# Attribute gathers that add onto cleared places, 52 of them ahead of the first network's gathers

## The reference, cut to what matters

```
x = _layernorm(x + _L0_gnn_ref(x, ...))   # graph transformer, two layers, per-edge attention
x = _layernorm(x + _L1_gnn_ref(x, ...))   # attention by leaky_relu, summed by source node
x = _layernorm(x + _L2_gnn_ref(x, ...))   # two hypergraph convolutions (four hops)
x = _layernorm(x + _L3_gnn_ref(x, edge_attr_4, edge_attr_10, ...))
```

```
out0 = alpha * (einsum(s0 * a0, w_00_0) + inv_sqrt3 * einsum(s1, a1, w_11_0))
out1 = alpha * (einsum(s0, w_01_1, a1) + einsum(s1 * a0, w_10_1))
messages = concat([out0, out1]) * msg_rad
agg = segment_sum(messages, edge_dst)
```

## Time and profile before

| | before |
|---|---|
| median of three runs | 5668.25 us |
| the profiled execution, its own time | 5646.56 us |
| its span | 5645.4 us |
| busy PE, DVE, ACT, POOL | 3618.7, 2869.4, 1858.3, 3438.4 us |
| mean granted TensorE clock | 0.81 |

### The profile page before, as it was taken

One profiled execution on the slowest core, in us unless ns is written; L12 is line 12 of the kernel. 1 busy time (PEld: TensorE's weight loads), 2 busy tenths in 40 slices (PEclk: granted clock), 3 DMA queues, 4 the chain that ended last, 5 costly groups with the idle time before them and its releaser, 6 DMA issues.

```text
span 5645.4 us, 59886 instructions
## 1 busy us (share of the span) xinstructions
PE 3618.7 (64%) x15291; PEld 2680.2 (47%) x15291; DVE 2869.4 (51%) x6725; ACT 1858.3 (33%) x5462; POOL 3438.4 (61%) x3085
## 2 busy tenths in 40 slices
PE   4554443667964444599794666621116999968887
PEld 3433232445653232366563444411005888767776
DVE  6465567886434454788532667622002322434445
ACT  1243344663333343577231111100001010146655
POOL 4466667888886666788887666677771000046664
PEclk8876677998986666799896888865558999979988
DMA  7688885663258888576424666621004878846665
GB/s 259 198 288 279 281 289 152 161 161 50 22 119 276 287 278 288 134 169 141 71 20 76 174 168 179 173 31 20 11 11 142 262 228 276 251 142 178 178 175 141
DMA packets 688351, 951.03 MB, mean 168 GB/s; under 512 B 230789, under 2 KB 479668, under 8 KB 687880
## 3 DMA queue, kind: packets, MB, share of 16 engines
q1 hardware_dynamic: 419634, 538.30, 31.0%
q0 software_dynamic: 251600, 385.84, 28.1%
q10 hardware_dynamic: 16774, 23.00, 1.2%
HBM read 727.03 MB, written 219.80 MB: 168 GB/s over the span
## 4 chain that ended last, share of the span: by engine, by line
issue 26%; PE 23%; POOL 19%; DVE 11%; another core or an unknown queue 10%; DMA 6%; SPq 3%; ACT 1%; DVEq 1%; ACTq 0%; POOLq 0%
PE bank L2650 10%; POOL arena L927 6%; POOL sc L950 6%; POOL ATT L964 6%; PE bank L2775 6%; PE bank L2772 4%; DMA ATT<-arena 3%; DMA sc<-arena 2%; SPq L620 2%; DVE arena L1376 2%; DVE arena L1746 2%; DVE arena L1466 2%; DVE arena L1352 1%; PE bank L2490 1%
## 5 line engine op out<-in xcount | busy, mean ns | idle before, releaser
L927 POOL DMA_INDIRECT arena<-KVT,arena x832 | 801.4, 963 | 480.5 <-issue 280.3
L2490 PE MATMUL bank<-arena 128*128 128x264 f32 x1664 | 598.5, 512 | 659.8 <-issue 366.1
L927 POOL DMA_INDIRECT arena<-YT,arena x416 | 405.7, 975 | 932.6 <-DMA YT<-arena 721.6
L2490 PEld LDWEIGHTS bank<-arena 128*128 128x128 f32 x1664 | 384.9, 248 | 872.8 <-issue 663.6
L964 POOL DMA_INDIRECT ATT<-arena x391 | 644.1, 1647 | 125.1 <-issue 110.0
L950 POOL DMA_INDIRECT sc<-arena x391 | 641.6, 1641 | 125.1 <-issue 111.5
L1466 DVE TENSOR_TENSOR arena<-arena,bank 128x256 f32<-128x256 f32 x832 | 297.5, 413 | 564.5 <-remote 360.9
L927 POOL DMA_INDIRECT arena<-X1T,arena x416 | 412.0, 990 | 243.5 <-issue 126.1
L2447 PE MATMUL bank<-arena 128*128 128x273 f32 x1664 | 455.1, 412 | 141.5 <-DVE arena L1525 94.5
L2631 PE MATMUL bank<-arena 128*128 128x261 f32 x832 | 315.8, 530 | 293.9 <-DVE arena L1376 158.2
L980 POOL DMA_INDIRECT arena<-ATTR,arena x416 | 416.4, 1001 | 139.7 <-issue 139.7
(11 more groups left out here) (333 smaller groups left out, 6661.0 us busy)
## 6 DMA issues: line engine op xcount, KB each, us to landing
VE<-arena SPq DMA_DIRECT2D x208, 512.0 KB
arena<-VE SPq DMA_DIRECT2D x208, 512.0 KB
left<-ATT SPq DMA_DIRECT2D x250, 320.0 KB
left<-AM SPq DMA_DIRECT2D x250, 320.0 KB
ATT<-arena POOLq DMA_DIRECT2D x25, 1600.0 KB, 6.6
arena<-LOCT SPq DMA_DIRECT2D x312, 128.0 KB
arena<-ATT SPq DMA_DIRECT2D x75, 384.0 KB
AM<-arena SPq DMA_DIRECT2D x100, 256.0 KB
```

The lines of the kernel that those rows point to most:

```text
L927: GP.indirect_dma_start(out=ring[:, i % n, k, :], out_offset=None, in_=table, in_offset=bass.IndirectOffsetOnAxis(ap=idx[:, 4 * i + k:4 * ...
L2490: mm = P.matmul(b_[:, 0:264], OHQ[:, i % 3, k * 128:(k + 1) * 128], QS[:, i % 4, k, :], start=True, stop=True)
```

## The change

Every attribute gather becomes an adding one (`compute_op=ALU.add`) with a bounds check. For this DVE clears columns 2 to 5 of `PA` once, right after the edge number has been copied out of column 2. The gathers are cut in two: the first 52 columns are issued before POOL's waits for l1, behind the 391 counting DMAs; the other 364 stay where all 416 were.

```diff
+EARLY = 52
@@ pool_engine
+        def add_attributes(cols):
+            for c in cols:
+                GP.indirect_dma_start(
+                    out=PA[:, c, 2:6], out_offset=None, in_=ATTR,
+                    in_offset=bass.IndirectOffsetOnAxis(ap=PA[:, c, 0:1].bitcast(I), axis=0), bounds_check=R1 - 1,
+                    compute_op=ALU.add).then_inc(attr_back.sem, 16)
+
+        GP.wait_ge(*attr_out(1))
+        add_attributes(range(EARLY))
         GP.wait_ge(*index_made("l1", 1))
         GP.wait_ge(*acc_clear("l1", 1))
...
             gather("l1", i, X1T, 72, idst, o_ring)
 
-        GP.wait_ge(*attr_out(1))
-        for c in range(T):
-            GP.indirect_dma_start(
-                out=PA[:, c, 2:6], out_offset=None, in_=ATTR,
-                in_offset=bass.IndirectOffsetOnAxis(ap=PA[:, c, 0:1].bitcast(I), axis=0)).then_inc(attr_back.sem, 16)
+        add_attributes(range(EARLY, T))
         GP.wait_ge(*acc_clear("l3", 1))
@@ vector_engine
         d.then(V.tensor_copy(PA[:, :, 0].bitcast(I), PA[:, :, 2]))
+        d.mark(V.memset(PA[:, :, 2:6], 0.0))
```

## The result

| | before | after |
|---|---|---|
| time, median | 5670.16 us (5663.96 to 5679.35, 4 runs) | 5281.32 us (5277.41 to 5286.17, 4 runs) |
| ratio | | 0.9313, 95% interval 0.9297 to 0.9330 |
| profiled execution, span | 5646.56, 5645.4 us | 5281.95, 5280.8 us |
| mean granted clock of TensorE | 0.810 | 0.832 |
| POOL busy | 3438.4 us | 3684.8 us |

The forecast was 5331 us, in a range of 5220 to 5500.

A forecast was written before the change was run, and what follows sets the result against it. Plain attribute gathers issued without pause were taken to stall handoffs in l1's tail and a0. The terms -470 + 97 + 35 + 1 = -337 us, against the median 5668.25, gave 5331 us, range 5220 to 5500.

The forecast's parts named there:

- Part 1: l1's tail: the last 24 additions no longer stall, 38 us instead of 148.5, gain 110 us.
- Part 2: a0 with the first fifth of hop 0: 100 us unstalled instead of 460, gain 360 us.
- Part 3: Ahead of l1: 52 adding gathers at 1.86 us, hidden by nothing, cost 97 us (70 to 102).
- Part 4: Beside the hops: 364 gathers at 1.93 us, done 141 us before Y, hidden; binding from 2.3 us each.
- Part 5: In the hops: the gathers' DMA traffic beside the hops' loads costs 35 us, between nothing and 110.
- The low end of the cost: In the hops: no delay, if a gather into SBUF costs the DMA a fifth of a scatter into DRAM.
- Part 6: Before the first k group: DVE's memset costs 1 us (0 to 2); the bounds check costs nothing.
- A: Before Y: POOL or the DMA rings become the bound; at 2.6 us a gather 5472 us; chance 0.09.
- B: From l1's tail on: gathers without waits between them stall, so it lasts longer, 5860 or 5913 us; chance 0.12.
- C: l1's tail and a0: adding gathers cost POOL 1.34 us and stall like plain ones, 5668 us; chance 0.03.
- D: l1's tail and a0: the stall only shrinks, 470 us becomes 235, whole time 5565 us; chance 0.04.

The follow-up runs named there:

- e5: Kernel before with five small POOL memsets ahead of each plain gather, no add, nothing early: 5228.7 us.
- e4: Changed kernel with all 416 adding gathers late, none ahead of l1, on the second chip: 5189.4 us, ratio 0.9189 to the kernel before.
- e3: Kernel before with each plain attribute gather waiting for the landing of the one four before: 5671.0 us.
- e7: Kernel before with its 416 plain gathers held back until a0 is over, second chip: 5694.1 us against 5644.7, ratio 1.0080.
- e10: Kernel before with each plain attribute gather waiting for the landing of the one right before it, third chip: 5319.0 us, 531 over the kernel before.

## Why the prediction was right

**The mechanism.** Right that nobody waited for work in those 600 us (the products and copies waited for were done, only PE's signals of it came some 30 us late), that the attribute gathers caused it, and that making them add would end it. e1, the same kernel without the add, is 5678 against 5281. Wrong in what it took for the cause: "plain gathers issued without pause stall the handoffs, and adding ones don't" joins two things, and e5 shows that plain ones do no such harm at 1.54 us. That the two kinds differ on these chips was read rightly; that it is the add that makes the difference was a guess that came out well, because the add also slows POOL. What both cures have in common is the slower pace, 1.96 and 1.54 us against 1.34. It is not shown that the pace is the cause: the memsets also put other work between the gathers, and the runs that were to part the two ran where nothing stalls. Where the edge lies is open. One reading was off: over the five full stretches of the stall PE was busy 11 to 21%, not 15 to 20, and DVE 7 to 25%, not 16; no term of the sum rests on it.

**Part 1, l1's tail.** -120 us against -110. **Part 2, a0.** -357 against -360; the working from one undisturbed part (100 us) met 103.7.

**Part 3, the early gathers.** 96.4 against 97: the undisturbed spacing of the counting adds was the right row.

**Part 4, the late gathers.** Hidden, as said, but with less to spare: 1.98 us each against 1.93, the last at 4528.5, Y 84 us behind where 141 were forecast. e4 showed the bound that part 4 warned of.

**Part 5, contention.** The term that was mis-sized: +35 expected, +1.4 measured. The DMA queues of the kernel after from 3953 to 4060, and SP's wait from 3950 to 4600:

```profile
q1 hardware_dynamic: 13508, 30.75, 88.8%
q0 software_dynamic: 7632, 0.11, 11.1%
```

```profile
SPq L787 <- PE bank L2657: 371.4, 365, 3.7
```

A gather makes 7632 / 55 = 139 packets, as foreseen, but 11.1% of 107 us over 55 gathers is 0.22 us of the whole DMA each, not the 0.38 of the scatters into DRAM. So 88.8 + 11.1% just fills the engines (with PE at 100%), where 0.38 would have asked for more than there is; from 4090 to 4250 their share is 0.89. The loads also had room: from 3950 on SP waited 371 us for PE to free a place in the ring, so a late load was made up; PE waited 2.5 us in sum for left blocks, not 35. The low end of the cost was the true one, though not by the condition that the prediction set for it: a gather cost the DMA over half of a scatter, not a fifth. For the low end it had named the Trainium skill's page "DMA: Bandwidth & Descriptors", section "Anatomy of one DMA"; no run here shows the write receipts apart from the rest. By the other section, "Issuing engines are not separate DMA queues", the engines are indeed shared, as the two shares add up to 99.9%, but shared is not yet late.

**Part 6.** The memset took 1.45 us against 1; with it the start grew by 5.0 us up to the last counting add, the rest unassigned.

With the tail and a0 at -477, the early gathers at 96, contention at 1 and the memset at 1, the sum would read -378 against -365 measured; the other +13 is in the start, l1's gathers and the end, which a single execution of each doesn't resolve. The forecast of 5331 lay 50 us over the measured 5281. Of these, 28 are the sum (-337 against -365), and 22 the difference between the profiled execution and the median, which was carried over and wasn't there in the kernel after.

**The rivals.** A (POOL or the DMA bind) didn't come; POOL's 1.96 us stayed under 2.3. B fell with e3. C's arithmetic (70 us come ahead, 70 us of stall go) is what e1 did, within 12 us. D: nothing of the stall is left, apart from "remote" waits of up to 6.4 us while l1's gathers still run.

What the prediction couldn't see from one trace is that the stall doesn't belong to the kernel alone: on a third chip its premise is missing.

## What to carry to other kernels

When all engines slow down together, TensorE's clock falls with them and waits are put down to "remote" in equal portions (here 11 us), look for the one engine that goes on at its full pace, and try to slow that one down: five idle memsets ahead of each gather were worth 7.7% where the gathers stalled the core (one execution), and cost nothing where they didn't. Then compare, for one handoff after another, when the work ended and when the next engine took it: that names the engine whose signals are late, which the word "remote" doesn't. A change that buys such a cure with work on the critical path (52 gathers, 96 us) can pay only where the stall exists, and by the estimate above it loses 2% on the third chip; time it on more than one chip before it is kept. Work moved beside a stage that is bound elsewhere is free until its own engine is the last, and one subtraction in the timeline says when that is.

## What was not expected of the hardware

- On two of three chips, beside plain indirect gathers of 16 bytes a row, one per 1.34 us, PE's signals reach ACT some 30 us after its work is done (a0) and SP and DVE 67 to 79 us after (hops, e7), while DVE follows ACT after 0.04 us. SP then issues one load per 14.0 us. At 1.54 us (plain, with memsets between) a0 runs as after the change. On the third chip one per 1.36 us does nothing.
- The same kernel before took 5666, 5645 and 4788 us on three chips, 18% apart, at mean clocks of 0.81, 0.81 and 0.88. Nearly all of it lies beside plain gathers: l1's 416 take 654 us on the first and 541 on the third.
- An adding gather into SBUF costs POOL 1.96 us on the mean (1.85 ahead of l1, 1.98 beside the hops) against 1.34 for the plain one. It makes 139 packets instead of 32 and takes 0.22 us of the whole DMA's time, where the plain one takes 0.07 and the adding scatter into DRAM 0.38.
- A POOL that waits for the landing of each plain 128-row gather issues one per 3.19 us: 0.96 for the instruction and 2.2 of waiting (e10, third chip).
